# Routing tables of a two-layer mixture-of-experts kernel, built from 16-bit operands with the group as innermost axis

## The chip, the cores and the metric

The kernel runs on one core of one Trainium2 chip. The metric is device time in microseconds (us) of one launch. Five engines work side by side: TensorE (PE in the profile, its weight loads PEld), VectorE (DVE), ScalarE (ACT), GpSimd (POOL) and SyncE (SP), which only issues transfers. They meet through semaphores.

## The reference, cut to what matters

Two layers work on x of 16 x 128 rows of 256 numbers. The part that the change touches is the routing of each layer's mixture of experts: every row picks its best two of 8 experts, each (row, choice) gets a place in its expert's list, and the rows are gathered in that order.

```python
top_vals, top_idx = jax.lax.top_k(probs, K)                  # K = 2, E = 8
flat_idx = top_idx.T.reshape(-1)                             # 4096 (choice, row) pairs
onehot = jax.nn.one_hot(flat_idx, E, dtype=jnp.int32)
cum = jnp.cumsum(onehot, axis=0) - 1
loc = jnp.take_along_axis(cum, flat_idx[:, None], axis=1)[:, 0]
keep = loc < C                                               # C = 640, layer 0 only
buf = jnp.zeros((E, C + 1, h), x.dtype).at[e_flat, l_flat].set(xk)
hid = jnp.einsum('ech,ehf->ecf', buf[:, :C], W_in)
a, g = jnp.split(hid, 2, axis=-1)
out_e = jnp.einsum('ecf,efh->ech', jax.nn.gelu(a, approximate=False) * g, W_out)
```

Layer 1 does the same without the limit C, with a SiLU in place of the gated GELU.

## The kernel before

All of it is one hand-written program per engine; there is no scheduler. The order on each engine is the order of the code, and semaphores tie the engines together.

The 4096 pairs stand as 128 partitions x 32 groups (`NG`). Once VectorE knows the place of every pair (`pick`, a whole number: its lowest 7 bits are the digit within a tile of 128, the rest says which of `NA` = 46 tiles), the list has to be turned round: which row stands at each place. The kernel does that by a product on TensorE. VectorE's `maps` writes three tables in 16-bit floats: `oha`, the one-hot of the tile (32 x 46 per partition), `by_slot`, the same times the pair's own number (`slot_wide`, a table filled once at the start), and `ohb`, the one-hot of the digit (32 x 128), in four parts of 8 groups. TensorE's `invert` then does 32 matmuls, one for each group, that add up in one bank of PSUM: `ohb` of the group is the stationary operand (128 columns), and the 92 columns of `by_slot` and `oha` of the group stream through. Eight matmuls wait for each part of `ohb`. From the result `turned_slots` makes the row numbers, and GpSimd gathers rows with them (`gather0`, line 518; `gather1`, line 585), ten transfers for the first two experts of layer 0.

What stands around this in layer 0, in program order: VectorE goes from `maps` to a few small operations (lines 1149 to 1153), `value_gates(0)` (1137), `turned_slots` (1114 and 1115) and the targets (1158 to 1161). TensorE fills the time before `invert` with `busy(9)` (line 1540, dummy matmuls whose result nobody reads), and after it does `value_gates(1)` (16 matmul records of 8 columns) and `values(1)` (16 of 256 columns), both on line 1515. ScalarE copies the values out (`values_out(1)`, line 686); this frees the bank for `xt0`, the transposes of the gathered rows (line 1696), with more `busy` fillers between them. ScalarE and VectorE split the turned rows into high and low parts (lines 741 and 1207), and the expert's matmuls start (line 1684). The gathers also wait until the normalised rows lie in memory (`xn_rows`, SyncE line 444).

In layer 1, TensorE does `busy(24)` ahead of `invert(1)`, and the gathers (line 585) wait for the row numbers and for the last quarter of the normalised rows (line 475), which ScalarE writes at line 664 and before which it works out the gates (lines 882 to 891), some from a product made by GpSimd (line 574).

Of the kernel before, what the change touches and what calls it, by code (L numbers as in the profile page):

```python
# [20 lines left out]
ALU = mybir.AluOpType  # L21
# [5 lines left out]
F16 = mybir.dt.float16  # L27
# [47 lines left out]
CB_W = 2 * P  # L75
MAP_PARTS = 4
MAP_BLOCKS = 2


def constants():  # L80
# [24 lines left out]
def build(nc, x, ctxt, mask, g_xattn, g_ffn, wg0, w_in, w_out, wq, bq, wk, bk, wvT, wv, bvc, bv, wg1T, w1, w2, cf_d, out):  # L105
    with ExitStack() as ctx:
        def sb(name, shape, dt=F32):
            return ctx.enter_context(nc.sbuf_tensor(name, shape, dt))
# [12 lines left out]
        slot_wide = sb("slot_wide", [P, NG, NA], F16)  # L121
        xs = sb("xs", [P, NB, D])
        cx = sb("cx", [P, NB, D])
        cT_all = sb("cT_all", [P, DC, T])
# [50 lines left out]
        rhs_a = xflat[:, 0:MAP_BLOCKS * NA * NG // 2].bitcast(F16).rearrange("p (g a) -> p g a", g=NG)  # L175
        by_slot, oha = (rhs_a[:, :, n * NA:(n + 1) * NA] for n in range(MAP_BLOCKS))
        ring = sb("ring", [P, NG * NA])
        ga = ring[:, 0:4 * HALF].rearrange("p (n c) -> p n c", n=4)
        ohb = flat(ys[:, :, :])[:, 0:NG * P // 2].bitcast(F16).rearrange("p (g n) -> p g n", g=NG)
# [37 lines left out]
        def c(name):  # L217
            return cf[:, CF[name][0]:CF[name][1]]
# [759 lines left out]
        def _(dve):  # L978
            links = [0]

            def link(ins):

                links[0] += 1
                ins.then_inc(chain, 1)
                dve.wait_ge(chain, links[0])
# [59 lines left out]

            norm0(0)
            dve.wait_ge(cf_in, 16)
            link(dve.tensor_copy(slot_wide[:, :, :], c("slot").unsqueeze(2).broadcast_to([P, NG, NA])))
            coefs(0, 0)
            dve.wait_ge(tanh_ready, 1)  # L1050
            retained(0)
# [65 lines left out]

            slot, real = (PD[:, 0, 128 + n * NA:128 + (n + 1) * NA] for n in range(MAP_BLOCKS))

            def maps(layer, high_slot):  # L1120

                dve.tensor_tensor(oha, high_slot.unsqueeze(2).broadcast_to([P, NG, NA]),
                                  c("iota_a").unsqueeze(1).broadcast_to([P, NG, NA]), ALU.is_equal)\
                    .then_inc(oha_ready, 1)
                dve.wait_ge(oha_ready, layer + 1)
                dve.tensor_tensor(by_slot, oha, slot_wide[:, :, :], ALU.mult)\
                    .then_inc(slot_ready, 1)
                for n in range(MAP_PARTS):
                    at = slice(n * NG // MAP_PARTS, (n + 1) * NG // MAP_PARTS)
# [18 lines left out]
            maps(0, sm[:, 3, :])  # L1148
# [355 lines left out]
        def _(pe):  # L1504
# [153 lines left out]
            def invert(layer):  # L1658

                pe.wait_ge(slot_ready, layer + 1)  # L1660
                for g in range(NG):
                    if g % (NG // MAP_PARTS) == 0:
                        pe.wait_ge(map_ready, layer * MAP_PARTS + g // (NG // MAP_PARTS) + 1)
# [268 lines left out]
def flat(ap):  # L1932
    return ap.rearrange("p a b -> p (a b)")
# [33 lines left out]
```

## Time and profile before

| | us |
|---|---|
| median of 3 runs | 570.64 |
| lowest and highest run | 569.64, 571.45 |
| span of the profiled execution | 573.6 |
| TensorE busy | 532.9 (93%) |
| VectorE busy | 335.6 (59%) |
| ScalarE busy | 321.8 (56%) |
| GpSimd busy | 251.9 (44%) |

The profiled execution's span, from its first to its last instruction, is 573.6 us. It is one execution, and it is 3.0 us above the median of the runs. TensorE is at work nearly all the time, so a microsecond anywhere else counts only where TensorE waits for it, or where TensorE itself works at the lower of its two clocks (2.4 and 1.2 GHz; the profile gives the granted share, 1.0 or 0.5).

### The profile page before, as it was taken

Reading aid. Unit: us, or ns where it says so; the run is one execution under the profiler, and the core shown is the slowest. Engines: PE = TensorE matmul, PEld = TensorE weight load, DVE = VectorE, ACT = ScalarE, POOL = GpSimd, SP = SyncE. Lnnn points to the kernel's source line nnn. Section 1 sums busy time; section 2 is a strip of 40 time slices with the busy share of each in tenths; the row PEclk is TensorE's granted clock in tenths of the full one; section 3 lists DMA queues with packets and bytes.
Section 4 is the critical chain, followed back from the end, with each engine's and each line's share of the span. In section 5 each row is a group of like instructions: output and inputs, shape, how many; then the busy total and the mean of one; then the engine's idle time right before and its main releaser. Section 6 shows DMA issues by size and latency. Waiting matters only on the chain.

```text
span 573.6 us, 12551 instructions
## 1 busy us (share of the span) xinstructions
PE 532.9 (93%) x4079; PEld 508.9 (89%) x4080; DVE 335.6 (59%) x796; ACT 321.8 (56%) x670; POOL 251.9 (44%) x284
## 2 busy tenths in 40 slices
PE   2899889999999999998996989999999999999993
PEld 1789789999999999986785879999999999999993
DVE  2888845765655675475677865464626463543631
ACT  3573345665656675435577646565646574654742
POOL 2400366664455542314000354556565546654654
PEclk9997699999999999979999899999999999999998
DMA  8944253445245443362033343644454545362333
GB/s 251 382 172 149 74 160 105 152 153 169 91 152 172 119 160 110 119 221 75 0 110 129 77 157 69 191 118 113 113 122 96 143 110 119 48 193 45 42 51 44
DMA packets 52454, 72.76 MB, mean 127 GB/s; under 512 B 7200, under 2 KB 43936, under 8 KB 52416
## 3 DMA queue, kind: packets, MB, share of 16 engines
q1 hardware_dynamic: 40752, 50.34, 26.7%
q0 software_dynamic: 11664, 21.94, 17.2%
q8 instruction: 20, 0.33, 0.2%
q14 instruction: 18, 0.15, 0.1%
HBM read 51.54 MB, written 20.73 MB: 126 GB/s over the span
## 4 chain that ended last, share of the span: by engine, by line
PE 80%; DVE 9%; DMA 4%; ACT 3%; issue 2%; POOL 1%; DVEq 0%; SPq 0%; POOLq 0%; ACTq 0%
PE PA L1684 27%; PE PD L1684 18%; PE PC L1684 17%; PE PB L1515 3%; PE PC L1515 2%; PE PD L1515 2%; PE PB L1696 2%; DMA xg<-xn_rows,row_x 2%; PE PB L1873 2%; DVE stats L990 1%; DMA cx<-ctx 1%; PE PA L1515 1%; PE PA L1549 1%; PE PB L1509 1%; DVE xs L1043 1%
## 5 line engine op out<-in xcount | busy, mean ns | idle before, releaser
L1684 PE MATMUL PA<-xhi,whi 128*128 128x256 f32 (+1 forms) x440 | 128.6, 292 | 4.2 <-issue 2.1
L1684 PE MATMUL PA<-xhi,wlo 128*128 128x256 f32 (+1 forms) x440 | 125.8, 286 | 0.0
L1684 PE MATMUL PA<-xlo,whi 128*128 128x256 f32 (+1 forms) x440 | 125.7, 286 | 0.0
L1250 DVE TENSOR_TENSOR hlo<-cT_all,hhi 128x512 fp32r<-128x512 f32 x78 | 54.2, 694 | 111.8 <-ACT hhi L937 111.7
L935 ACT ACTIVATE cT_all<-PA 128x512 f32<-128x512 f32 x78 | 46.6, 597 | 93.2 <-PE PA L1684 93.1
L609 POOL DMA_INDIRECT out<-ys,row_o x38 | 63.5, 1670 | 75.6 <-DVE ys L1456 41.5
L1684 PEld LDWEIGHTS PA<-xhi,whi 128*128 128x128 f32 x440 | 84.2, 191 | 5.6 <-issue 4.5
L1684 PEld LDWEIGHTS PA<-xlo,whi 128*128 128x128 f32 x440 | 84.2, 191 | 0.0
L1684 PEld LDWEIGHTS PA<-xhi,wlo 128*128 128x128 f32 x440 | 84.1, 191 | 0.0
L1684 PE MATMUL PD<-whi,hhi 128*128 128x256 f32 x284 | 81.1, 285 | 0.4 <-DVE wlo L1202 0.4
L1684 PE MATMUL PD<-whi,hlo 128*128 128x256 f32 x284 | 80.4, 283 | 0.0
L1684 PE MATMUL PD<-wlo,hhi 128*128 128x256 f32 x284 | 80.3, 283 | 0.0
L518 POOL DMA_INDIRECT xg<-xn_rows,row_x x45 | 46.3, 1028 | 66.9 <-DVEq L1116 39.9
L527 POOL DMA_INDIRECT y_rows<-ys,row_y x40 | 41.8, 1045 | 55.5 <-ACT ys L762 53.3
L585 POOL DMA_INDIRECT xg<-xn_rows,row_x x44 | 50.4, 1145 | 23.0 <-POOL slot_gate L603 8.4
L1684 PEld LDWEIGHTS PD<-whi,hhi 128*128 128x128 f32 x284 | 54.5, 192 | 0.6 <-issue 0.6
L1684 PEld LDWEIGHTS PD<-wlo,hhi 128*128 128x128 f32 x284 | 54.5, 192 | 0.0
L1684 PEld LDWEIGHTS PD<-whi,hlo 128*128 128x128 f32 x284 | 54.5, 192 | 0.0
L937 ACT ACTIVATE hhi<-cT_all 128x512 fp32r<-128x512 f32 x78 | 49.2, 631 | 2.5
L1250 DVE TENSOR_TENSOR wlo<-raw,whi 128x512 fp32r<-128x512 f32 x64 | 40.5, 686 | 11.2 <-ACT whi L804 11.1
L1684 PE MATMUL PC<-whi,hhi 128*128 128x256 f32 x160 | 45.3, 283 | 0.0
L1684 PE MATMUL PC<-wlo,hhi 128*128 128x256 f32 x160 | 45.3, 283 | 0.0
(269 smaller groups left out, 1205.6 us busy)
## 6 DMA issues: line engine op xcount, KB each, us to landing
raw<-w SPq DMA_DIRECT2D x16, 1024.0 KB, 5.7
raw<-L_ffn_W_in SPq DMA_DIRECT2D x8, 1024.0 KB, 5.2
raw<-L_ffn_W_out SPq DMA_DIRECT2D x8, 512.0 KB
y_rows<-ys SPq DMA_DIRECT2D x8, 512.0 KB, 8.0
xn_rows<-xn SPq DMA_DIRECT2D x8, 512.0 KB, 3.5
xs<-x SPq DMA_DIRECT2D x4, 512.0 KB, 6.5
cx<-ctx SPq DMA_DIRECT2D x4, 512.0 KB, 7.0
ys<-y_rows SPq DMA_DIRECT2D x4, 512.0 KB, 4.6
```

The source lines that it names most:

```text
L518: pool.indirect_dma_start(xg[:, s, :], None, xn_rows[0].ap(), bass.IndirectOffsetOnAxis(ap=row_x[:, e % E * CT + t:e % E * CT + t + 1], ax ...
L527: pool.indirect_dma_start(y_rows.ap(), bass.IndirectOffsetOnAxis(ap=row_y[:, e * CT + t:e * CT + t + 1], axis=0), ys[:, s, :], None).then_ ...
L585: pool.indirect_dma_start(xg1[j % SLOTS1], None, xn_rows[1].ap(), bass.IndirectOffsetOnAxis(ap=row_x[:, j:j + 1], axis=0)).then_inc(g1_in[ ...
L609: pool.indirect_dma_start(out, bass.IndirectOffsetOnAxis(ap=row_o[:, j:j + 1], axis=0), ys[:, j % SLOTS1, :], None, compute_op=ALU.add).th ...
L935: act.activation(group1(h1, g), PA[:, g % 2, :], ACT.Silu).then_inc(silu_done, 1)
L937: act.activation(group1(hhi, g), group1(h1, g), ACT.Copy).then_inc(h1_hi, 1)
L990: ins = dve.bn_stats(stats[:, b, :], xs[:, q * QB + b, :])
L1250: return dve.tensor_tensor(dst, src, hi.bitcast(F32), ALU.subtract)
L1515: mm = pe.matmul(dst, a, b, start=(k == 0), stop=(k == len(lhs) - 1))
L1684: mm = pe.matmul(dst, a[k], b[k], start=(first and k == 0 and a is lhs_hi and b is rhs_hi), stop=(last and k == n - 1 and a is lhs_lo))
L1696: mm = pe.transpose(bank0(pair)[:, t - tiles_of(pair)[0], k, :], xg[:, s, k * P:(k + 1) * P], ident)
L1873: mm = pe.transpose(PB[:, par, k * WIDE1 + t * P:k * WIDE1 + (t + 1) * P], xg1[s][:, k * P:(k + 1) * P], ident)
```

## The change

The three tables get another layout and other operands. The 32 groups are cut into 4 parts of 8 (`PART`), and within a part the group becomes the innermost axis: `ohb` is now part x 128 digits x 8 groups, and `oha` and `by_slot` are part x 46 tiles x 8 groups. All operands of the comparisons are 16-bit floats: the digit (`low16`), the tile (`high16`), the pair's number (`slot16`), and a table of the numbers 0 to 127, each written eight times in a row (`number_table`), which takes the place of `slot_wide` and of the 32-bit constants `iota` and `iota_a`. The digit is no longer cut out of the whole number with a bit operation but worked out as place minus 128 times tile, which writes 16 bits directly. On TensorE, both operands of the 32 matmuls are now read with 16 bytes from one column to the next (every eighth 16-bit number), where they were dense.

```diff
+        number_table = sb("number_table", [P, P, PART], F16)
+        slot16, low16, high16 = (sb(n, [P, NG], F16) for n in ("slot16", "low16", "high16"))
...
-            link(dve.tensor_copy(slot_wide[:, :, :], c("slot").unsqueeze(2).broadcast_to([P, NG, NA])))
+            dve.tensor_copy(number_table[:, :, :], c("iota").unsqueeze(2).broadcast_to([P, P, PART]))
+            link(dve.tensor_copy(slot16[:, :], c("slot")))
...
-                link(dve.tensor_scalar(smi[:, 1, :], smi[:, 0, :], P - 1, None, ALU.bitwise_and))
                 link(dve.tensor_scalar(smi[:, 2, :], smi[:, 0, :], 7, None, ALU.arith_shift_right))
+                link(dve.scalar_tensor_tensor(low16[:, :], smi[:, 2, :], -float(P), smi[:, 0, :], ALU.mult, ALU.add))
...
-                dve.tensor_tensor(oha, high_slot.unsqueeze(2).broadcast_to([P, NG, NA]),
-                                  c("iota_a").unsqueeze(1).broadcast_to([P, NG, NA]), ALU.is_equal)\
-                    .then_inc(oha_ready, 1)
+                dve.tensor_tensor(oha, over_parts(high16), number_table[:, 0:NA, :].unsqueeze(1)
+                                  .broadcast_to([P, MAP_PARTS, NA, PART]), ALU.is_equal).then_inc(oha_ready, 1)
...
-                dve.tensor_tensor(by_slot, oha, slot_wide[:, :, :], ALU.mult)\
-                    .then_inc(slot_ready, 1)
+                dve.tensor_tensor(by_slot, oha, over_parts(slot16), ALU.mult).then_inc(slot_ready, 1)
...
-                    dve.tensor_tensor(ohb[:, at, :], smi[:, 1, at].unsqueeze(2).broadcast_to([P, NG // MAP_PARTS, P]),
-                                      c("iota").unsqueeze(1).broadcast_to([P, NG // MAP_PARTS, P]), ALU.is_equal)\
+                    dve.tensor_tensor(ohb[:, n, :, :], low16[:, n * PART:(n + 1) * PART].unsqueeze(1)
+                                      .broadcast_to([P, P, PART]), number_table[:, :, :], ALU.is_equal)\
                         .then_inc(map_ready, 1)
...
-            link(dve.tensor_tensor(sm[:, 3, :], sm[:, 1, :], sm[:, 2, :], ALU.add))
+            link(dve.tensor_tensor(high16[:, :], sm[:, 1, :], sm[:, 2, :], ALU.add))
...
-            maps(1, smi[:, 2, :])
+            link(dve.tensor_copy(high16[:, :], smi[:, 2, :]))
+            maps(1)
...
-                    mm = pe.matmul(PD[:, 0, 128:128 + MAP_BLOCKS * NA], ohb[:, g, :], rhs_a[:, g, :], start=(g == 0),
-                                   stop=(g == NG - 1))
+                    mm = pe.matmul(PD[:, 0, 128:128 + MAP_BLOCKS * NA],
+                                   ohb[:, g // PART, :, g % PART], rhs_a[:, g // PART, :, g % PART],
+                                   start=(g == 0), stop=(g == NG - 1))
```

On VectorE, layer 1, from the reduction that gives the place of each pair (`smi`) to the row numbers, before:

```order
L1107 TENSOR_REDUCE smi<-loc 128x32
L1108 TENSOR_SCALAR smi<-smi 128x32
L1109 TENSOR_SCALAR smi<-smi 128x32
L1122 TENSOR_TENSOR xg<-smi,cf 128x32x46
L1126 TENSOR_TENSOR xg<-xg,slot_wide 128x32x46
L1130 TENSOR_TENSOR ys<-smi,cf 128x1024 x4
L1114 CAST row_y<-PD 128x46
L1115 TENSOR_SCALAR row_x<-row_y 128x46
```

The same place after. `xg` and `ys` are the buffers in which `oha` with `by_slot` and `ohb` lie.

```order
L1111 TENSOR_REDUCE smi<-loc 128x32
L1112 TENSOR_SCALAR smi<-smi 128x32
L1113 SCALAR_TENSOR_TENSOR low<-smi 128x32
L1385 CAST high<-smi 128x32
L1129 TENSOR_TENSOR xg<-high,number_table 128x4x368
L1132 TENSOR_TENSOR xg<-xg,slot 128x4x368
L1134 TENSOR_TENSOR ys<-low,number_table 128x1024 x4
L1118 CAST row_y<-PD 128x46
L1119 TENSOR_SCALAR row_x<-row_y 128x46
```

The tables have as many elements as before and stand at the same place; one small cast is added ahead of them in this layer. In layer 0 the count of instructions there stays the same, and at the start of the program one fill of 1472 elements becomes one of 1024 and one of 32. TensorE's order does not change.

## Rows read from the trace of the kernel before

**Rows 1.** The page: engines' busy time, and TensorE's granted clock in 40 slices.
```profile
PE 532.9 (93%) x4079; PEld 508.9 (89%) x4080; DVE 335.6 (59%) x796; ACT 321.8 (56%) x670; POOL 251.9 (44%) x284
PEclk9997699999999999979999899999999999999998
```

**Rows 2.** Chain that ended last, 46 to 80 us: start, length, what.
```profile
55.03 1.70 DVE xg L1122
...
56.76 0.93 DVE xg L1126
57.69 4.55 DVE ys L1130 x4
...
62.29 0.80 PE PD L1664 x8
63.08 3.35 PE PA L1515 x16
66.44 5.58 PE PC L1515 x16
...
72.04 1.03 ACT vv L686
...
76.33 2.02 PE PA L1684 x12
```

**Rows 3.** The table instructions: duration ns min/median/max, first and last start, forms.
```profile
L1122 DVE TENSOR_TENSOR xg<-sm,cf x1: 1692/1692/1692, 55.0 to 55.0; 128x1472 f16<-128x1472 f32 x1
L1126 DVE TENSOR_TENSOR xg<-xg,slot_wide x2: 926/927/928, 56.8 to 318.5; 128x1472 f16<-128x1472 f16 x2
L1130 DVE TENSOR_TENSOR ys<-smi,cf x8: 1217/1219/1221, 57.6 to 322.8; 128x1024 f16<-128x1024 int32 x8
```

**Rows 4.** Timeline of TensorE around `invert(0)`; in brackets the idle time before.
```profile
55.56 2.17 PE L1540 MATMUL PC<-cf 128*128 128x128 f32 x18
...
58.97 0.49 PE L1664 MATMUL PD<-xg,ys 128*128 128x92 f16 x8 [1.24 <-DVE ys L1130]
```

**Rows 5.** Matmuls on bf16 and f16 operands: duration ns min/median/max.
```profile
L1664 PE MATMUL PD<-xg,ys x64: 201/205/287, 59.0 to 324.4; 128*128 128x92 f16 x64
...
L1652 PE MATMUL PD<-oh,cb x2: 283/352/421, 52.1 to 311.2; 128*128 128x256 bf16 x2
...
L1654 PE MATMUL PD<-cum,cb x2: 183/200/217, 52.4 to 312.0; 128*128 128x8 bf16 x2
```

**Rows 6.** By windows: us, busy PE, PEld, DVE, ACT, POOL, granted clock, DMA share, GB/s.
```profile
60.00:60.50 0.50, 0.49 (x8) 0.49 (x8) 0.50 (x1) 0.50 (x1) 0.00 (x0) 0.64 1.10 391
...
70.00:70.50 0.50, 0.50 (x3) 0.41 (x2) 0.43 (x3) 0.00 (x0) 0.19 (x2) 0.62 0.21 57
...
244.00:246.00 2.00, 2.00 (x14) 2.00 (x13) 1.08 (x2) 1.99 (x5) 0.00 (x0) 0.61 0.65 199
```

**Rows 7.** Chain: the same kinds of matmul at the full clock.
```profile
43.36 3.68 PE PC L1515 x32
...
252.71 3.45 PE PC L1515 x16
```

**Rows 8.** Timeline: row numbers, first and third gather, third tile's transposes; landing times of line 518.
```profile
63.92 0.19 DVE L1115 TENSOR_SCALAR row_x<-row_y 128x46 int32<-128x46 int32 x1
...
64.46 1.14 POOL L518 DMA_INDIRECT xg<-xn_rows,row_x  x1 [39.91 <-DVEq L1116]
...
67.89 0.95 POOL L518 DMA_INDIRECT xg<-xn_rows,row_x  x1 [0.30 <-issue]
...
74.50 0.38 PE L1696 MATMUL PB<-cf,xg 128*128 128x128 f32 x2
...
DMA to landing us min/median/max: 2.7/2.8/6.9
```

**Rows 9.** Last write of the normalised rows of layer 0, and transfers of that stretch.
```profile
58.77 0.36 SPq L444 DMA_DIRECT2D xn_rows<-xn  x1
...
xn_rows<-xn SPq DMA_DIRECT2D x1, 512.0 KB, 2.7
```

**Rows 10.** Layer 1: timeline rows, and the chain around the last write of the rows.
```profile
316.83 1.72 POOL L574 TENSOR_TENSOR nmr<-mv,rstd 128x4 f32<-128x4 f32 x1 [5.44 <-ACT rstd L657]
...
322.04 1.39 PE L1664 MATMUL PD<-xg,ys 128*128 128x92 f16 x24
...
324.83 0.19 DVE L1115 TENSOR_SCALAR row_x<-row_y 128x46 int32<-128x46 int32 x1
...
318.82 2.07 ACT xn L664 x4
...
320.91 4.40 DMA xn_rows<-xn
```

More of the change, by code:

```diff
@@ L77 @@
 MAP_BLOCKS = 2
+PART = NG // MAP_PARTS
 def constants():
@@ L120, in build @@
         warm = sb("warm", [P, 2])
-        slot_wide = sb("slot_wide", [P, NG, NA], F16)
+        number_table = sb("number_table", [P, P, PART], F16)
+        slot16, low16, high16 = (sb(n, [P, NG], F16) for n in ("slot16", "low16", "high16"))
         xs = sb("xs", [P, NB, D])
@@ L174, in build @@
         xg1 = [xflat[:, n * DG:(n + 1) * DG] for n in range(SLOTS1)]
-        rhs_a = xflat[:, 0:MAP_BLOCKS * NA * NG // 2].bitcast(F16).rearrange("p (g a) -> p g a", g=NG)
-        by_slot, oha = (rhs_a[:, :, n * NA:(n + 1) * NA] for n in range(MAP_BLOCKS))
+        rhs_a = xflat[:, 0:MAP_BLOCKS * NA * NG // 2].bitcast(F16)\
+            .rearrange("p (m a g) -> p m a g", m=MAP_PARTS, g=PART)
+        by_slot, oha = (rhs_a[:, :, n * NA:(n + 1) * NA, :] for n in range(MAP_BLOCKS))
         ring = sb("ring", [P, NG * NA])
         ga = ring[:, 0:4 * HALF].rearrange("p (n c) -> p n c", n=4)
-        ohb = flat(ys[:, :, :])[:, 0:NG * P // 2].bitcast(F16).rearrange("p (g n) -> p g n", g=NG)
+        ohb = flat(ys[:, :, :])[:, 0:NG * P // 2].bitcast(F16).rearrange("p (m n g) -> p m n g", m=MAP_PARTS, n=P)
         inv = ring[:, 4 * HALF:4 * HALF + 4 * NA].rearrange("p (n a) -> p n a", a=NA)
@@ L1118, in _, with maps, over_parts @@
             slot, real = (PD[:, 0, 128 + n * NA:128 + (n + 1) * NA] for n in range(MAP_BLOCKS))
-            def maps(layer, high_slot):
-                dve.tensor_tensor(oha, high_slot.unsqueeze(2).broadcast_to([P, NG, NA]),
-                                  c("iota_a").unsqueeze(1).broadcast_to([P, NG, NA]), ALU.is_equal)\
-                    .then_inc(oha_ready, 1)
+            def maps(layer):
+                def over_parts(x):
+                    return x[:, :].rearrange("p (m g) -> p m g", g=PART).unsqueeze(2).broadcast_to([P, MAP_PARTS, NA, PART])
+                dve.tensor_tensor(oha, over_parts(high16), number_table[:, 0:NA, :].unsqueeze(1)
+                                  .broadcast_to([P, MAP_PARTS, NA, PART]), ALU.is_equal).then_inc(oha_ready, 1)
                 dve.wait_ge(oha_ready, layer + 1)
-                dve.tensor_tensor(by_slot, oha, slot_wide[:, :, :], ALU.mult)\
-                    .then_inc(slot_ready, 1)
+                dve.tensor_tensor(by_slot, oha, over_parts(slot16), ALU.mult).then_inc(slot_ready, 1)
                 for n in range(MAP_PARTS):
-                    at = slice(n * NG // MAP_PARTS, (n + 1) * NG // MAP_PARTS)
-                    dve.tensor_tensor(ohb[:, at, :], smi[:, 1, at].unsqueeze(2).broadcast_to([P, NG // MAP_PARTS, P]),
-                                      c("iota").unsqueeze(1).broadcast_to([P, NG // MAP_PARTS, P]), ALU.is_equal)\
+                    dve.tensor_tensor(ohb[:, n, :, :], low16[:, n * PART:(n + 1) * PART].unsqueeze(1)
+                                      .broadcast_to([P, P, PART]), number_table[:, :, :], ALU.is_equal)\
                         .then_inc(map_ready, 1)
@@ L1145, in _ @@
             link(dve.scalar_tensor_tensor(sm[:, 2, :], eidx[:, :], float(CT), smi[:, 2, :], ALU.mult, ALU.add))
-            link(dve.tensor_tensor(sm[:, 3, :], sm[:, 1, :], sm[:, 2, :], ALU.add))
+            link(dve.tensor_tensor(high16[:, :], sm[:, 1, :], sm[:, 2, :], ALU.add))
             dve.wait_ge(zero_out, 16 * K * NQ)
-            maps(0, sm[:, 3, :])
+            maps(0)
             link(dve.tensor_tensor(lg[:, :, :], lg[:, :, :], top[:, :, 0:1].broadcast_to([P, NB, E]), ALU.subtract))
@@ L1661, in invert @@
                 for g in range(NG):
-                    if g % (NG // MAP_PARTS) == 0:
-                        pe.wait_ge(map_ready, layer * MAP_PARTS + g // (NG // MAP_PARTS) + 1)
-                    mm = pe.matmul(PD[:, 0, 128:128 + MAP_BLOCKS * NA], ohb[:, g, :], rhs_a[:, g, :], start=(g == 0),
-                                   stop=(g == NG - 1))
+                    if g % PART == 0:
+                        pe.wait_ge(map_ready, layer * MAP_PARTS + g // PART + 1)
+                    mm = pe.matmul(PD[:, 0, 128:128 + MAP_BLOCKS * NA],
+                                   ohb[:, g // PART, :, g % PART], rhs_a[:, g // PART, :, g % PART],
+                                   start=(g == 0), stop=(g == NG - 1))
                 mm.then_inc(map_done, 1)
```

## The prediction

> **What bounds the kernel now.** The page comes first: TensorE is busy 93% of the span, VectorE 59% [rows 1]. A faster VectorE instruction therefore counts only where TensorE waits for it. The slices of TensorE's clock say more: of 40, the fourth and fifth (43 to 72 us) are at 0.7 and 0.6 of full speed, and the routing of layer 0 is in them [rows 1]. The chain that ended last, read from 46 to 80 us, then shows the changed instructions on the path one behind the other: 1.70 us for `oha`, 0.93 for `by_slot`, 4.55 for the four parts of `ohb`, the last eight matmuls of `invert` to 63.08; then TensorE's own work (3.35 and 5.58 us on line 1515), ScalarE's copy to 73.07, and the first expert's matmuls at 76.33 [rows 2]. In layer 1 the chain doesn't pass through the tables. It goes through ScalarE's last normalisation and its write to memory, 320.91 to 325.30 [rows 10], while the row numbers are done at 325.02 [rows 10]. The tables have 0.3 us of slack there.
>
> **VectorE's tables, layer 0.** Line 1126 has 1472 elements with all operands of 16 bits and takes 926 ns; line 1122 has as many with a 32-bit operand and takes 1692, line 1130 has 1024 and takes 1219 [rows 3]. The last two give 1.056 ns per element and 137 ns fixed; with the same fixed part, line 1126 runs at 0.536 ns, half of that. After the change all three are like line 1126. So `oha` goes from 1692 to 926 ns, 0.77 us less, and a part of `ohb` from 1219 to 137 + 1024 x 0.536 = 686, 0.53 less. A part took 4.55 / 4 = 1.137 us in the chain [rows 2] and takes 0.604; four save 2.13. `by_slot` stays. Together 2.90 us, 1.3 of them ahead of the first matmul. The number of small instructions ahead of the tables is the same in layer 0, with one line for another of its size; the fills at the start lie in VectorE's wait for the first coefficients. I cost both at nothing.
>
> What could be wrong in this is the new inner axis of eight, re-read for each digit. The Trainium skill (Vector Engine (DVE) Microarchitecture Reference, section 5.1, Performance modes) has a two-source instruction do two elements a cycle if all operands have 2 bytes and an innermost step of one with more than one element, a row that is read again included. By that rule the new forms qualify. Line 1126's row agrees for long rows; no row here has a row of eight that is re-read.
>
> **TensorE's matmuls.** Eight matmuls took 0.49 us at the full clock [rows 4], one takes 205 ns from start to end [rows 5]: (490 - 205) / 7 = 41 ns from one to the next. Now each column lies 16 bytes from the next, in both operands. The nearest row is line 1654, whose eight moving columns lie 64 bytes apart: 183 ns at best, against 283 for the 256 dense columns of line 1652 [rows 5]. At one column per clock of 2.4 GHz, 248 columns would make 103 ns and not 100, so the eight cost some 3 ns more, 0.42 a column: each column takes two clocks. By 41 ns for 92 columns (0.446 each) the 248 would make 111 ns, and a spaced column would cost 1.3 ns more. That bounds it: nothing more (41 ns a matmul) to 41 + 92 x 1.3 = 161 ns, or 207 if the 128 stationary columns set the pace (41 + 128 x 1.3). I take 41 + 92 x 0.42 = 80 ns, from the closer reading of the nearest row, and keep 41 and 207 as ends.
>
> Layer 0 then: the fillers end at 57.73 [rows 4]. Parts are ready at 55.03 + 0.95 + 0.95 + 0.60 = 57.53 and each 0.60 later, the last at 59.34. Eight matmuls take 0.64, so TensorE becomes the slower by a hair: 57.74 + 32 x 0.080 + 0.12 = 60.4, where it was 63.08. That is 2.7 us. At 41 ns it would be 59.8.
>
> **What is late next.** VectorE reaches the row numbers 2.9 us earlier, at 61.2. The gathers also wait for the last quarter of the normalised rows, issued at 58.77 and landed 2.7 us later, 61.47 [rows 9]. GpSimd then starts at about 61.65 where it started at 64.46 [rows 8]: 2.8 us earlier. The third gather started at 67.89 and lands 2.8 to 3.4 us later, 70.7 to 71.3; its transposes ran at 74.50 [rows 8]. So the gathers had over 3 us of slack, and TensorE was late on its own account: from 60.0 to 70.3 it had the lower clock [rows 6]. Before it fell, TensorE had done 0.49 us of work in the 2.3 us since its fillers [rows 4]. The same kinds of matmul at the full clock take 3.68 / 2 = 1.84 us for sixteen of 8 columns and 3.45 for sixteen of 256 [rows 7], where the chain has 3.35 and 5.58 [rows 2]: 3.6 us lost. With parts every 0.60 us, TensorE has hardly a gap from 55.5 to 60.4. **I take it that the clock stays up.** Then 60.3 + 1.84 + 3.45 = 65.6, ScalarE's copy to 66.7, and with the fillers between the tiles the third tile's turn comes 1.4 us after that, 68.1. Its rows land at 70.7 to 71.3 less 2.8, so 67.9 to 68.5. Both arrive together, 6.2 us before 74.50. Splitting follows as before. The gain of layer 0 is about 6.2 us against the profiled execution, and from there on TensorE carries it to the end.
>
> In runs without the profiler the fall may come a little later and the cold stretch be shorter, since the phase between clock and program isn't fixed by the program; the span lies 3.0 us above the median. So I take 5.6 us off the median, 4.8 to 6.6.
>
> **Layer 1.** VectorE's tables end 2.7 us earlier (2.90 less the added cast of 0.2), but TensorE is in its 24 fillers until 322.04 [rows 10]. All parts are ready by then, so `invert` takes 32 x 0.080 + 0.12 = 2.7 us, to 324.7, where it ended at 324.56; the row numbers are at about 325.2, still under the 325.30 at which the rows have landed. This costs nothing up to 81 ns a matmul, and 32 ns for each nanosecond above. GpSimd's small product of line 574 took 1.72 us beside line 1122 [rows 10] and so was held until 318.55; ScalarE is in its own gates until 318.82, so neither a faster nor an equal wait shows.
>
> **The rivals.**
> *The clock falls all the same.* The 1.84 us of 8-column matmuls behind `invert` are thin work: at 244 to 246 us, in 32 of the same kind, the granted share fell to 0.61 although TensorE was busy throughout [rows 6]. And with everything earlier, TensorE waits for the gathers between 65.6 and 69.7 with fillers alone. A fall at the old place leaves only the tables' gain, 2.7 us: 567.9. A fall in the wait for the gathers costs 1.1 to 1.7 us of 5.6: 566.4, inside the first case's range.
>
> *Spaced reads are slow.* This is the one that ends on the other side. With the clock as it was, layer 0 gains 63.08 - 57.74 - 0.12 = 5.2 us less 32 matmuls, and layer 1 loses 32 matmuls less 2.6 us (325.3 - 0.55 - 0.12 - 322.04). The two cancel at 7.8 / 64 = 122 ns a matmul. At the upper bound of 161 ns the kernel is 2.5 us slower, 573.1; at 207 it is 5.4 us slower, 576. For it speaks the 1.3 ns reading of line 1654; against it the other reading of the same row, on which the forecast rests. The Trainium skill (Advanced Engine Details and Errata, Memory Cachelines) speaks against this change: lines of SBUF have 16 bytes, and full rate needs at least two hits on each; here every column is on a line of its own. It gives no price. By the page alone the direction is this rival's; the row of line 1654 shows a price near 0.42 ns a column, by which it stays hidden.
>
> *Short rows stop the fast form.* If rows of eight run at the old rate, each table takes what it took, and 80 ns a matmul hides under 1.14 us a part: 570.6, no change. That is also what a change that doesn't do what it says looks like.
>
> **How the numbers follow.** The clock stays up: 0.55, 565.0 (564.0 to 565.8, down to 562.5 with cheap matmuls and a longer cold stretch before). Only the tables' gain: 0.22, 567.9. Slow spaced reads: 0.13, of which 0.03 still a little faster, 0.03 about equal, 0.07 slower. No fast form: 0.06. Something not named, either side: 0.04. Faster by over 0.3% (1.7 us, about what a measurement of this kernel can tell from no change): 0.55 + 0.22 + 0.03 + 0.02 = 0.82; within it 0.03 + 0.06 = 0.09; slower 0.07 + 0.02 = 0.09. The range reaches from 562.5 over the second case to 569.5, just short of no change.
>
> **What would show it.** In the profile after: the comparison into `xg` at 926 ns and the parts of `ohb` at 686; TensorE's 32 matmuls in layer 0 without gaps, 8 in about 0.75 us; the granted share 1.0 from 54 us on through the values; ScalarE's copy of the values starting near 65.7; the first expert's matmul near 70 where it was 76.33; in layer 1 the first gather still set by the landing of the rows. The forecast is wrong if a matmul takes over 80 ns, if the clock falls near 60 us, or if the third gather lands later than 68.5.

## The result, and the profile after

The changed kernel is slower. Its median is 578.98 us (574.19 to 580.45, 4 runs), beside 570.14 us (568.21 to 571.45, 4 runs) for the kernel before in the same comparison: ratio 1.013, 95% interval 1.0088 to 1.0172, so 5.0 to 9.8 us. (The ratio is an estimate of its own and not the quotient of the two medians, which is 1.0155.) Forecast were 565.0 us and a range of 562.5 to 569.5.

The page of the kernel after: engines' busy time, and TensorE's granted clock in 40 slices of the span, which is 577.6 us. The same execution is 579.45 us in the list of runs: a run's time is 1.8 to 2.0 us longer than its span in every kernel here. The span before, 573.6 us, is therefore about 575.5 us of a run, 5 us above the median and not the 3.0 us of the table before the prediction.

```profile
PE 545.3 (94%) x4079; PEld 521.4 (90%) x4080; DVE 328.2 (57%) x798; ACT 321.7 (56%) x670; POOL 249.0 (43%) x284
...
PEclk9995699999999999979999799999999999999997
```

Against [rows 1], VectorE is busy 7.4 us less and TensorE 12.4 us more, with the same number of matmuls. Which instructions those are, the durations say (ns, min/median/max, then the first and last start):

```profile
L1129 DVE TENSOR_TENSOR xg<-high,number_table x2: 925/926/926, 53.6 to 319.8; 128x1472 f16<-128x1472 f16 x2
...
L1134 DVE TENSOR_TENSOR ys<-low,number_table x8: 684/685/687, 55.5 to 323.4; 128x1024 f16<-128x1024 f16 x8
...
L1669 PEld LDWEIGHTS PD<-xg,ys x64: 141/145/153, 59.8 to 330.0; 128*128 128x128 f16 x64
L1669 PE MATMUL PD<-xg,ys x64: 327/350/358, 59.9 to 330.2; 128*128 128x92 f16 x64
```

The tables do what was forecast to the nanosecond: 926 for 1692 ns and 685 for 1219 [rows 3]. The 64 matmuls of `invert` don't: one takes 350 ns from start to end, where it took 205 [rows 5]. The chain of layer 0 shows the pace from one to the next:

```profile
56.44 3.67 PE PC L1545 x18
60.10 5.44 PE PD L1669 x32
65.54 3.27 PE PA L1520 x16
68.81 5.92 PE PC L1520 x16
...
79.05 2.02 PE PA L1690 x12
```

32 matmuls in 5.44 us are 170 ns each; before, eight took 0.49 us [rows 4], which is 41 ns each after the 205 ns of the first one. VectorE's tables are gone from the chain that ended last [rows 2]; TensorE stands in their place, and the first expert's matmul starts at 79.05 instead of 76.33. VectorE's own timeline shows the exchange: the last two parts of `ohb` end at 57.94, a few small operations follow until 59.2, and then the engine waits for TensorE.

```profile
56.66 1.29 DVE L1134 TENSOR_TENSOR ys<-low,number_table 128x1024 f16<-128x1024 f16 x2
...
65.58 0.20 DVE L1118 CAST row_y<-PD 128x46 int32<-128x46 f32 x1 [6.34 <-PE PD L1669]
```

The windows give TensorE's granted clock (the share behind the engines' busy times), here in layer 0 and in layer 1:

```profile
60.00:62.00 2.00, 2.00 (x14) 1.72 (x13) 0.00 (x0) 1.98 (x5) 0.00 (x0) 1.00 0.75 262
62.00:64.00 2.00, 2.00 (x13) 1.69 (x12) 0.00 (x0) 1.16 (x2) 0.00 (x0) 0.80 0.00 0
64.00:66.00 2.00, 2.00 (x14) 1.83 (x11) 0.39 (x2) 0.00 (x0) 0.00 (x0) 0.50 0.00 0
...
328.00:330.00 2.00, 2.00 (x14) 1.73 (x12) 0.00 (x0) 0.00 (x0) 0.00 (x0) 0.86 0.00 0
330.00:332.00 2.00, 2.00 (x12) 1.96 (x11) 1.16 (x5) 0.00 (x0) 0.65 (x1) 0.50 0.00 0
```

Two things are to be read in them. The clock falls in both layers while TensorE is busy without a gap in the slow matmuls (at 63.2 us in layer 0). And the pace hangs little on the clock, as windows with the 64 matmuls of line 1669 alone show: eight records in a microsecond at a share of 1.00, and eight at 0.50.

```profile
62.00:63.00 1.00, 1.00 (x8) 0.84 (x7) 1.00 0.00 0
...
64.00:65.00 1.00, 1.00 (x8) 0.87 (x6) 0.50 0.00 0
```

In layer 1 the fall is new: in the kernel before, the share was 1.00 in all windows from 320 to 338 us. One of these windows, and the 36 dummy matmuls behind `invert(1)`, before:

```profile
324.00:326.00 2.00, 1.95 (x22) 1.96 (x23) 1.15 (x5) 0.47 (x1) 0.00 (x0) 1.00 0.02 4
...
324.40 4.25 PE L1540 MATMUL PC<-cf 128*128 128x128 f32 x36
```

Layer 1 of the kernel after, in the chain, in GpSimd's and in TensorE's timeline:

```profile
325.12 5.45 PE PD L1669 x32
...
331.35 1.00 POOL L588 DMA_INDIRECT xg<-xn_rows,row_x  x1 [11.54 <-DVEq L1120]
...
330.38 5.38 PE L1545 MATMUL PC<-cf 128*128 128x128 f32 x36
```

`invert(1)` is on the path now. GpSimd's first gather waits for the row numbers (line 1120 is VectorE's), where it waited for the rows' write [rows 10], and the 36 dummy matmuls behind take 5.38 us where they took 4.25.

### The profile page after: what moved, and what is told of

It reads as the page before. It is cut to its first block, busy times and chain, and to the rows that moved or that the text cites. A ratio compares the mean times of both kernels' runs of the same rounds, so it can differ in the third digit from the quotient of the medians.

```text
span 577.6 us, 12553 instructions
## 1 busy us (share of the span) xinstructions
PE 545.3 (94%) x4079; PEld 521.4 (90%) x4080; DVE 328.2 (57%) x798; ACT 321.7 (56%) x670; POOL 249.0 (43%) x284
## 4 chain that ended last, share of the span: by engine, by line
PE 85%; DVE 9%; issue 2%; ACT 2%; DMA 1%; POOL 1%; DVEq 0%; SPq 0%
PE PA L1690 28%; PE PC L1690 18%; PE PD L1690 18%; PE PB L1520 3%; PE PC L1520 2%; PE PC L1545 2%; PE PD L1669 2%; DVE stats L993 2%; PE PD L1520 2%; PE PB L1702 2%; PE PA L1520 2%; PE PB L1879 2%; PE PB L1514 1%; DMA cx<-ctx 1%; DVE xs L1304 1%
## 5 line engine op out<-in xcount | busy, mean ns | idle before, releaser
L612 POOL DMA_INDIRECT out<-ys,row_o x38 | 63.4, 1669 | 73.9 <-DVE ys L1461 39.8
L530 POOL DMA_INDIRECT y_rows<-ys,row_y x40 | 41.8, 1046 | 55.4 <-ACT ys L765 53.3
L1690 PE MATMUL PC<-whi,hlo 128*128 128x256 f32 x160 | 45.3, 283 | 0.0
```

The lines of the kernel that those rows point to most:

```text
L530: pool.indirect_dma_start(y_rows.ap(), bass.IndirectOffsetOnAxis(ap=row_y[:, e * CT + t:e * CT + t + 1], axis=0), ys[:, s, :], None).then_ ...
L612: pool.indirect_dma_start(out, bass.IndirectOffsetOnAxis(ap=row_o[:, j:j + 1], axis=0), ys[:, j % SLOTS1, :], None, compute_op=ALU.add).th ...
L1690: mm = pe.matmul(dst, a[k], b[k], start=(first and k == 0 and a is lhs_hi and b is rhs_hi), stop=(last and k == n - 1 and a is lhs_lo))
```

## The experiments

Two theories stood first. *Moving*: the columns of the operand that streams through, 16 bytes apart, set the pace of 170 ns. *Stationary*: the weight loads of 128 columns 16 bytes apart do. After that the question was why dense operands with the fast tables bring so little.

All ratios below are against the kernel before on the same chip, whose medians there were 573.95 us (23 runs), 573.67 (19) and 573.86 (35), for the first four kernels, the next four and the last four. Each of the three groups ran on a chip of its own, so ratios of different groups are compared with more doubt than their intervals say. Times of single instructions come from one profiled execution of each kernel.

### Fast tables with dense operands

The layouts of the kernel before are kept. A value is written twice, so that the innermost axis of every comparison is a pair of 16-bit numbers.

```diff
-                dve.tensor_tensor(oha, high_slot.unsqueeze(2).broadcast_to([P, NG, NA]),
-                                  c("iota_a").unsqueeze(1).broadcast_to([P, NG, NA]), ALU.is_equal)\
-                    .then_inc(oha_ready, 1)
+                dve.tensor_tensor(oha.rearrange("p g (a t) -> p g a t", t=2), over(high2[:, :, :], NG, NA),
+                                  numbers(NG, NA), ALU.is_equal).then_inc(oha_ready, 1)
```

> Fast tables with dense reads on TensorE: the layouts of the kernel before, all operands of 16 bits, and each value that is spread over a row written twice, so that the innermost axis is a pair with a step of one. Theory A (the loss of the changed kernel is the spaced reads alone, and the rest of the prediction stands): comparisons at 926 and 686 ns, 41 ns from matmul to matmul in the product that inverts the list, no fall of the clock there, 4.8 to 6.6 us below the kernel before. Theory B (the clock falls behind the tables whatever they take): about 2.7 us below. Theory C (an innermost axis of two stops the fast form): comparisons at 1690 and 1219 ns, within 1 us of the kernel before.

572.24 us (568.75 to 575.22, 12 runs), ratio 0.9961, interval 0.9928 to 0.9994: faster, by less than half of the 4.8 to 6.6 us expected. A matmul takes what it took, and the tables are fast (926 and 684 ns). The duration row, and the chain:

```profile
L1679 PE MATMUL PD<-xg,ys x64: 202/204/208, 61.2 to 322.0; 128*128 128x92 f16 x64
...
57.89 3.47 PE PC L1555 x18
61.36 1.33 PE PD L1679 x32
62.70 1.76 PE PA L1530 x16
64.45 3.57 PE PC L1530 x16
```

From 61.4 us on the forecast holds: the clock is up, and `value_gates(1)` and `values(1)` take 1.76 and 3.57 us where they took 3.35 and 5.58 [rows 2]. But the dummies ahead ran at half clock, 3.47 us where they took 2.17 [rows 4], and ended 2 us after the tables (59.4). SyncE and GpSimd show what else was late, and the windows where the clock fell instead:

```profile
60.93 0.36 SPq L445 DMA_DIRECT2D xn_rows<-xn  x1
...
64.65 2.13 POOL L519 DMA_INDIRECT xg<-xn_rows,row_x  x1 [39.93 <-DMA xn_rows<-xn]
...
74.00:76.00 2.00, 2.00 (x11) 2.00 (x10) 0.47 (x1) 0.00 (x0) 1.64 (x2) 0.62 0.32 104
```

The gathers waited for the last quarter of the normalised rows, written at 60.93, and started where they had started before (64.65 against 64.46, [rows 8]). The next low stretch came after the first expert's start, which is at 73.49.

The dummies and the write were late for one reason: TensorE's clock, low from about 50 us on in both executions, rose at 60.8 here and at 53.3 in the kernel before. TensorE's program is the same up to the dummies, and its times agree to 0.1 us until there; the first matmuls that show the difference, before and here:

```profile
52.60 2.19 PE L1515 MATMUL PA<-wvg,cT_all 128*128 128x8 f32 x16
```

```profile
52.67 3.42 PE L1530 MATMUL PA<-wvg,cT_all 128*128 128x8 f32 x16
```

In the other traces this rise lies anywhere from 49 to 62 us. No run shows that the tables have to do with it, so how late the dummies and the write are can be a matter of the execution that was profiled.

### Spaced operands with slow tables

As after, with `low16` and `high16` in 32 bits.

```diff
-        slot16, low16, high16 = (sb(n, [P, NG], F16) for n in ("slot16", "low16", "high16"))
+        slot16, low16, high16 = (sb(n, [P, NG], F32 if n != "slot16" else F16) for n in ("slot16", "low16", "high16"))
```

> Spaced reads with slow tables: the changed kernel with the digit and the tile number kept in 32 bits, so that the comparisons run at one element a cycle. Theory A (spaced reads at some 170 ns a matmul set the pace): the matmuls start 1.2 us later than in the changed kernel in layer 0 and run at the same 170 ns; about 1.2 us above the changed kernel, 8 to 10 us above the kernel before. Rival (the fast tables themselves cost time by holding the port that VectorE shares with GpSimd): as fast as or faster than the changed kernel.

584.07 us (580.17 to 584.58, 4 runs), ratio 1.0157, interval 1.0098 to 1.0216. The chain of layer 0:

```profile
59.39 5.44 PE PD L1669 x32
```

The pace is 170 ns again with comparisons at 1692 and 1218 ns, so the tables' speed has no part in it.

### Only the moving operand spaced, and only the stationary one

Both start from the kernel after; the operand that is dense again gets the layout and the tables of the kernel with dense pairs.

```diff
                     mm = pe.matmul(PD[:, 0, 128:128 + MAP_BLOCKS * NA],
-                                   ohb[:, g // PART, :, g % PART], rhs_a[:, g // PART, :, g % PART],
+                                   ohb[:, g, :], rhs_a[:, g // PART, :, g % PART],
```

> Only the moving operand is spaced (92 columns, 16 bytes apart); the stationary one-hot is dense, both tables fast. Theory M (the moving columns set the pace, 1.84 ns each): about 170 ns from matmul to matmul, the time of the changed kernel. Theory S (the 128 stationary columns set it, 1.32 ns each): about 41 ns, the time of the kernel with pairs and dense reads. Neither: both add up, 80 to 130 ns.

```diff
                     mm = pe.matmul(PD[:, 0, 128:128 + MAP_BLOCKS * NA],
-                                   ohb[:, g // PART, :, g % PART], rhs_a[:, g // PART, :, g % PART],
+                                   ohb[:, g // PART, :, g % PART], rhs_a[:, g, :],
```

> Only the stationary operand is spaced (128 columns, 16 bytes apart); the moving one is dense, both tables fast. Theory M: about 41 ns from matmul to matmul, the loads hidden, and the time of the kernel with pairs and dense reads. Theory S: about 170 ns and the time of the changed kernel.

585.33 us (583.48 to 586.41, 4 runs), ratio 1.0191 (1.0135 to 1.0247) with the moving operand spaced; 573.1 us (567.71 to 575.37, 10 runs), ratio 0.9985 (0.995 to 1.0021) with the stationary one. Durations and the chain of layer 1, first of the moving, then of the stationary kernel:

```profile
L1679 PEld LDWEIGHTS PD<-xg,ys x64: 98/117/128, 62.3 to 335.8; 128*128 128x128 f16 x64
L1679 PE MATMUL PD<-xg,ys x64: 326/343/345, 62.4 to 335.9; 128*128 128x92 f16 x64
...
331.02 5.27 PE PD L1679 x32
```

```profile
L1677 PEld LDWEIGHTS PD<-xg,ys x64: 143/164/175, 58.5 to 321.4; 128*128 128x128 f16 x64
L1677 PE MATMUL PD<-xg,ys x64: 204/236/242, 58.7 to 321.5; 128*128 128x92 f16 x64
...
319.78 1.95 PE PD L1677 x32
```

165 ns a matmul with the moving operand alone, 61 with the stationary one alone, 170 with both. The moving operand sets the pace. A spaced load has a price too, 164 ns from start to end where a dense one has 97 (145 with both operands spaced), but most of it lies beside the matmuls. The times don't tell the kernel with the moving operand spaced from the kernel after (1.0191 and 1.013, intervals that overlap), as *Moving* has it.

### Other distances

Parts of 4 groups (`MAP_PARTS = 8`) put the columns of both operands 8 bytes apart, parts of 2 groups (`MAP_PARTS = 16`) 4 bytes; in a third kernel the moving columns alone lie 64 bytes apart.

```diff
-MAP_PARTS = 4
+MAP_PARTS = 8
```

> The changed kernel with eight parts of four groups in place of four of eight: a column lies 8 bytes from the next, both operands. VectorE does eight comparisons of 512 elements (about 411 ns each) for four of 1024. Theory L (what costs is a new 16-byte stretch for every column): two columns fall in one stretch, so about 41 to 61 ns a matmul, and the time of the kernel with pairs and dense reads, within 1 us. Rival G (any gap between columns costs the same): 163 to 170 ns and the changed kernel's time. Rival H (the cost follows the distance): about 100 ns, 3 us above the kernel before.

> Sixteen parts of two groups: a column lies 4 bytes from the next. Theory L: 41 to 61 ns a matmul. Rival G: 163 to 170 ns. Rival H: about 70 ns.

```diff
-            .rearrange("p (m a g) -> p m a g", m=MAP_PARTS, g=PART)
+            .rearrange("p (a g) -> p a g", g=NG)
```

> Only the moving operand is spaced, by 64 bytes in place of 16 (the distance of the eight columns of the small bf16 matmul from which the prediction took its price). Theory L (each column on a stretch of its own, whatever the distance): 163 to 170 ns a matmul, as with 16 bytes. Rival (the distance matters, and that row was cheap because of it): about 80 ns, or above 200.

574.58 us (569.94 to 577.33, 10 runs), ratio 1.0015 (0.9976 to 1.0054) at 8 bytes; one run of 571.01 us at 4 bytes, one of 585.3 at 64. The chain of layer 1, at 8, 4 and 64 bytes:

```profile
319.09 2.77 PE PD L1669 x32
```

```profile
320.18 1.37 PE PD L1669 x32
```

```profile
329.96 5.02 PE PD L1682 x32
```

That is 87, 43 and 157 ns a matmul. None of the three theories on record had the 87 ns of 8 bytes: the first one's 41 to 61 ns were those of no loss with two columns on 16 bytes. For a matmul of 92 columns:

| distance of the moving columns | ns a matmul | ns a column |
|---|---|---|
| 2 bytes (dense pairs) | 42 | 0.46 |
| 4 bytes | 43 | 0.47 |
| 8 bytes | 87 | 0.95 |
| 16 bytes | 165 to 170 | 1.8 |
| 64 bytes | 157 | 1.7 |

At 4 bytes there are four columns on 16 bytes and nothing is lost; at two columns the pace is half; at one a quarter; farther apart costs no more. The rows fit a price of some 1.8 ns for every stretch of 16 bytes that is touched, as much as four columns take. In the kernels at 4 and 8 bytes the stationary columns lie as far apart too; but even at 16 bytes those alone make a matmul 61 ns and not 87.

The kernel at 8 bytes is also a test of the forecast as a whole, since 87 ns is close to the 80 that it was built on. In its trace the clock stays up from 53.3 until past 84 us, the values are copied at 65.76 us (forecast: near 65.7), and the first expert starts at 71.74 instead of 76.33:

```profile
65.76 1.02 ACT L689 ACTIVATE vv<-PC 128x1024 f32<-128x1024 f32 x1 [3.17 <-PE PC L1520]
```

By the prediction's terms it should have been over 4 us faster than the kernel before (its eight parts of `ohb` take 0.6 us more than four, and layer 1 loses 0.2). No gain shows: the ratio is 1.0015, and the lower end of its interval 0.9976.

The Trainium skill (Advanced Engine Details and Errata, Memory Cachelines) says that full performance needs at least two hits on a line of 16 bytes. The direction and the 16 bytes agree with these rows; two hits don't suffice here, since at 8 bytes a matmul takes 87 ns and not 42.

### Spaced operands in layer 1 alone

Layer 0 as in the kernel with dense pairs, layer 1 as after.

```diff
-                    mm = pe.matmul(PD[:, 0, 128:128 + MAP_BLOCKS * NA], ohb[:, g, :], rhs_a[:, g, :], start=(g == 0),
-                                   stop=(g == NG - 1))
+                    lhs, rhs = ((ohb[:, g, :], rhs_a[:, g, :]),
+                                (ohb_s[:, g // PART, :, g % PART], rhs_s[:, g // PART, :, g % PART]))[layer]
+                    mm = pe.matmul(PD[:, 0, 128:128 + MAP_BLOCKS * NA], lhs, rhs, start=(g == 0), stop=(g == NG - 1))
```

> Fast tables in both layers, dense reads in layer 0 (pairs), spaced reads (16 bytes) in layer 1 alone. In the profiles the first matmul of layer 1's experts stands 3.2 us later in the changed kernel than in the kernel before, counted from the fillers ahead of the product, and 1.7 us of it are taken up by the next gather, which TensorE then no longer waits for. Theory A (layer 1 loses only what is left of that): 1 to 3 us above the kernel with pairs and dense reads. Rival (the clock falls in layer 1's product as well and the loss stands in full): 4 us or more above it.

578.09 us (574.67 to 582.11, 10 runs), ratio 1.0081 (1.0038 to 1.0124). The ratio of the kernel with dense pairs in both layers is 0.9961, so spacing in layer 1 alone costs 1.2%, 6.9 us (about 4 to 10 by the two intervals together). The chain and a window:

```profile
320.98 5.42 PE PD L1709 x32
326.40 6.54 PE PC L1583 x36
...
326.00:328.00 2.00, 2.00 (x12) 1.98 (x11) 1.31 (x5) 0.00 (x0) 0.80 (x1) 0.50 0.00 0
```

The matmuls take 4.1 us more (5.42 less 1.33 to 1.35). The clock fell during them (at 324.7), and the 36 dummies behind, 4.25 us before, take 6.54: 2.3 us more. Together 6.4.

The windows of layer 1 of all kernels agree on the clock. In each of the five with moving columns 16 or 64 bytes apart there, the granted share fell to 0.50 before `invert(1)` had ended. In none of the nine others did it fall during `invert(1)`; in two of those, the one with 8 bytes and the last one below, it fell about 8 us after its end.

### Rows written earlier, fewer dummies, both, and both with slow tables

These start from the kernel with dense pairs. One moves ScalarE's last normalisation of layer 0 ahead of `context_out(1)`, for which it waited 8.0 us; one halves the dummies ahead of `invert(0)`; one does both; the last does both to the kernel before, with its slow tables.

```diff
+            normalise1(3)
             context_out(1)
-            normalise1(3)
...
-            busy(9)
+            busy(4)
             invert(0)
```

> The dense fast tables of e1_pairs, with ScalarE's last normalisation of layer 0 (normalise1(3)) moved ahead of its context_out(1), on which it waited 8 us for TensorE; so the last quarter of the normalised rows is written some microseconds earlier than 60.9. Theory G: the first gather follows the row numbers (63.2 in e1_pairs) and no longer the landing (64.65), the first expert matmul comes 1 to 1.5 us earlier, and the time is 1 to 1.5 us below e1_pairs, 3 to 4 us below before (ratio 0.993 to 0.995). Rival F: the dummies are the bound and the gathers had slack: within 0.5 us of e1_pairs. Rival C: the clock falls over the waiting stretch whatever comes earlier, and the gain shows in the profile at the first expert matmul but not in the time.

> The dense fast tables of e1_pairs with half the dummy matmuls ahead of the inversion in layer 0: busy(4) where it was busy(9). In the profile of e1_pairs the tables ended 2 us before the dummies did (59.4 against 61.36), because the dummies ran at half clock. Theory G (after fast tables the gathers are bound by the landing of the last quarter of the normalised rows, written at 60.9 us and landed at 64.6, which no filler touches): the row numbers come 1 to 2 us earlier than in e1_pairs and wait in vain; time within 1 us of e1_pairs, so 1.5 to 2.5 us below before (ratio 0.996). Rival F (the dummies on the path are the bound): first gather and first expert matmul 1.5 to 2 us earlier, 3.5 to 4.5 us below before (ratio 0.993). Rival C (the dummies hold the clock up): a longer low stretch, 0 to 2 us slower than e1_pairs.

> Both edits: dense fast tables, normalise1(3) ahead of context_out(1), busy(4) in place of busy(9) in layer 0. Theory G: neither bound stands any longer, the inversion follows the tables (59.4) and the gathers follow it: first gather near 61.5 to 62, first expert matmul 2 to 3 us before that of e1_pairs (73.49), time 2 to 4 us below e1_pairs, 4 to 6 below before (ratio 0.990 to 0.993). Rival C (TensorE's clock takes it back): the first expert matmul is earlier but the low stretch after it is longer, and the time is within 1 us of e1_pairs.

> The kernel before with its slow tables, with both edits of the order alone: normalise1(3) ahead of context_out(1), and busy(4) in place of busy(9) in layer 0. It tells what the two edits bring without fast tables. Theory G (the slow tables are then the bound, since they end at 62.3 whatever the fillers do): the row numbers stay where they are (63.9), the gathers had only 0.3 us to gain, and TensorE idles longer ahead of the inversion: between 1 us below and 1.5 us above before (ratio 0.998 to 1.003). Rival (the order alone makes the gain of e11_pairs_both): the same time as e11_pairs_both.

| | median us (lowest, highest; 12 runs each) | ratio to before (95%) |
|---|---|---|
| rows earlier | 570.8 (567.71, 572.45) | 0.9938 (0.9913 to 0.9963) |
| fewer dummies | 572.19 (568.89, 575.45) | 0.9972 (0.9946 to 0.9999) |
| both | 573.26 (568.95, 576.22) | 0.9992 (0.9962 to 1.0022) |
| both, slow tables | 575.31 (573.29, 578.64) | 1.0032 (1.0003 to 1.0061) |

The kernel with the rows written earlier has the lowest ratio of all, 3.6 us below the kernel before (3.1 by the medians). Its profiled execution took 570.61 us, about its median. GpSimd's first gather, ScalarE's copy of the values and TensorE's first expert matmul in it, then ScalarE's first two gelus:

```profile
61.80 1.14 POOL L519 DMA_INDIRECT xg<-xn_rows,row_x  x1 [37.15 <-DVEq L1122]
...
65.48 1.02 ACT L687 ACTIVATE vv<-PC 128x1024 f32<-128x1024 f32 x1 [2.93 <-PE PC L1530]
...
70.10 0.41 PE L1699 MATMUL PA<-xhi,whi 128*128 128x320 f32 x1 [0.95 <-DVE xlo L1221]
...
73.79 0.44 ACT L751 ACTIVATE ring<-PA 128x320 f32<-128x320 f32 x1 [3.92 <-remote]
76.73 0.44 ACT L751 ACTIVATE ring<-PC 128x320 f32<-128x320 f32 x1 [2.50 <-remote]
```

The gathers follow the row numbers, the values are copied at 65.48 (forecast for the change: near 65.7), and the first expert matmul is at 70.10 (forecast: near 70), 6.2 us before that of the kernel before. The moved write has only a part in this: the clock rose at 53.6 us in this execution, and the dummies took 2.17 us and not the 3.47 of the trace with dense pairs alone. Then part of the 6.2 us goes again: the first two gelus wait 3.9 and 2.5 us for something that the profile calls remote, where in the kernel before both (78.39 and 80.14) followed TensorE's matmuls. What that is the trace doesn't tell. The moved write didn't bring it: the kernel with fewer dummies has the same two waits, of which the profile puts the first down to TensorE, whose twelve matmuls had ended 1.4 us before.

```profile
72.00 0.44 ACT L751 ACTIVATE ring<-PA 128x320 f32<-128x320 f32 x1 [3.63 <-PE PA L1699]
...
74.93 0.44 ACT L751 ACTIVATE ring<-PC 128x320 f32<-128x320 f32 x1 [2.49 <-remote]
```

The transposes of the second expert's rows (six on line 1711) start at 88.08 where they started at 92.38, so in the kernel with the rows written earlier 4.3 of the 6.2 us are left.

Fewer dummies bring nothing alone, and 0.5% is lost when the rows are early too (0.9938 against 0.9992, the intervals just touch), where the kernel with both was expected 4 to 6 us below the kernel before. This is so although in the trace with fewer dummies alone the rows were written at 55.99 us and the first expert started at 68.53, the earliest of all traces: that execution, of 568.98 us, was the second fastest of twelve whose median is 572.19. One trace's milestones are not the median's. The windows of the kernel with both:

```profile
60.00:64.00 4.00, 4.00 (x12) 3.28 (x13) 3.40 (x8) 0.00 (x0) 3.09 (x4) 0.50 0.22 66
...
72.00:74.00 2.00, 1.86 (x7) 1.87 (x8) 1.11 (x2) 0.00 (x0) 0.34 (x1) 0.50 0.35 88
```

The gathers start 2.6 us earlier than with the dummies kept (59.16), but the values and the first expert run at the lower clock. This is one execution; that dummies are what holds the clock up was not tried apart from it. The last kernel shows that both edits of the order bring nothing with slow tables, rather a loss. It doesn't show that the gain of the fastest kernel needs the fast tables: that one has the rows written earlier and all its dummies, and this was not tried with slow tables. Of the pair that differs in the tables alone, both edits with fast and with slow ones, the ratios are 0.9992 and 1.0032, with intervals that overlap.

## Why the prediction was wrong

**VectorE's tables: right.** 926 and 685 ns for forecast 926 and 686; the new inner axis of eight runs at the fast rate. VectorE's time is 7.4 us less, and TensorE stands in its place on the path.

**The pace of a spaced matmul: the step that failed first.** The prediction took 80 ns, with 41 and 207 as ends, and said that gain and loss cancel at 122. Measured are 170. It had read a spaced column's price from the eight columns of line 1654 [rows 5]: 0.42 ns more if the 248 other columns of line 1652 take 0.417 each, 1.3 more if they take 0.446. The two readings differ by 8 ns in a term of 103 or 111, and the remainder of 3 or 11 ns for eight columns was all that was left to see. The second reading was right: 0.45 to 0.46 ns is the dense pace of these matmuls and 1.7 to 1.8 the spaced one, 1.3 to 1.4 more. The prediction called the first one the closer reading, though its own 41 ns for 92 columns was the better measurement of a dense column. Only the bound of 161 was near.

**Layer 0.** It was to win 2.7 us in the matmuls and 3.6 from the clock. `invert(0)` ended at 65.54 instead of 63.08, the clock was low from 63.2 to 73.4 us where it had been from 60.1 to 70.4, and the first expert started 2.7 us later.

**Layer 1.** The prediction priced it at 32 ns for each nanosecond above 81: 2.8 us. Against the start of the dummies ahead (316.66 us, 2.8 later than in the trace before), `invert(1)` started 0.1 us later and ended 3.2 us later (330.57 against 324.56). That is about the price forecast. What the rival of slow reads left out is the clock: it took TensorE's clock as it was. In the kernel spaced in layer 1 alone, a third of the loss is the dummies behind at half clock. So even with 170 ns in its formula the rival would have said 3 us slower, and the measured loss is 5.0 to 9.8.

**The sum.** The ratios put it together: fast tables with dense operands -2.2 us (0.9961), spacing in layer 1 +6.9 (1.0081 less 0.9961), spacing in layer 0 the rest of 1.013, +2.8. The last is the least sure: it is the difference of two ratios from two chips whose intervals overlap. The traces have more for it, 5.6 us between the first expert's start with dense pairs (73.49) and after (79.05), and so has the kernel with the moving operand spaced in both layers (1.0191, which leaves 6.3). The pair of traces before and after shows only 4.0 us of span in all, since the profiled execution before was 5 us above its median.

**"The clock stays up": right in most traces, but its worth was the second step that failed.** In the two traces with fast tables whose clock rose where it had risen before (53.3 to 53.6 us), 8 bytes and rows earlier, it stayed up until past 84 us, where it had fallen at 60.1 before. At 4 bytes, in sixteen parts, it had risen at 50.8 and fell at 61.1, in the values. But of the 5.6 us that this and the tables were to bring, the ratios show 2.2 with dense pairs, and at 87 ns a matmul none that is clear of the noise. So the forecast would have missed its 565 us with its own 80 ns too. The traces point at three holes in the sum. The dummies and the rows' write, at 60.93 and no longer 58.77, are late when they fall in a low stretch; the prediction took the landing at 61.47 from one trace as if it were fixed, and it moves with ScalarE's wait for TensorE. The milestones came true to about 0.2 us in the trace with the write moved, which also had the early rise of the clock, and the time fell by 3.6 us. And about 2 of its 6.2 us were gone by the second expert, behind ScalarE's two waits, for which the prediction had no term. The third hole is the baseline: 5.6 us were read from one execution that was itself 5 us above the median. If the low stretch from 60.1 to 70.4 was longer there than in most executions, there was less to win. The kernel with both edits and slow tables speaks for it: its low stretch ended near 65 us, its first expert started at 71.60, 4.7 us before 76.33, and yet its median lies above that of the kernel before. The prediction took off 0.6 us for this; there is no second trace of the kernel before to tell.

**Still open:** what the two gelus wait for; how often the kernel before has the low stretch that was to be won back; how much of the 3.6 us is the moved write's, since 0.9938 and 0.9961 aren't told apart by their intervals; and why fewer dummies lose what the earlier rows win, since one execution shows where the clock was low but not what made it so.

## What to carry to other kernels

A layout that is good for VectorE is read by someone: count, for the operand that streams through TensorE, how many columns lie on 16 bytes, and keep four or more. The fast form of VectorE's comparisons needs only a pair as its innermost axis, so both can be had, by writing the small operand twice. When a price is read from the difference of two long durations, work out the price by the best measured rate and not by the nominal one, and let the forecast rest on the dearer reading if the sign of the result hangs on it. And before a low stretch of the clock is counted as something to win back, look at a second execution: the clock rose at 53.3 us in one and at 60.8 in another after the same matmuls.

## What the runs showed of the hardware

A moving column of 16 bits costs 0.46 ns at distances of 2 and 4 bytes, 0.95 at 8, 1.8 at 16 and 1.7 at 64. At 16 bytes it does so at either of the two clocks: in layer 0, where 32 matmuls took 5.44 us and the granted share went from 1.00 to 0.50 in the middle of them, eight records stand in a microsecond before the fall and eight after it. A stationary operand with 16 bytes between its columns makes a load 164 ns long instead of 97 (145 when the moving operand is spaced as well), and a matmul with its load 61 ns instead of 41. VectorE's fast form holds with an innermost axis of 8, 4 and 2 elements, one operand of which is re-read for each row: 685 ns for 1024 elements, 419 for 512, 282 for 256. And TensorE's granted clock fell to 0.50 during the 32 spaced matmuls of layer 1 in all five kernels that had them, with the engine busy 2.00 of 2.00 us in each window: busy time alone doesn't tell that the clock will stay.
